# An adaLN, recurrence and gated-RNN kernel in f32: three tiny tensors declared behind the weights, so that the weights begin at multiples of 128 bytes

## What is computed

```python
xb = jnp.einsum('bsd,ed->sbe', x, B)
def step(h, xb_t):
    h = jnp.tanh(h @ A.T + xb_t)
    return (h, h @ C.T)
out = jnp.transpose(ys, (1, 0, 2)) + x            # then normalised, * gamma + beta

def step(c, xt):
    ft = jax.nn.sigmoid(xt @ wf.T + c @ uf.T + bf)
    it = jax.nn.sigmoid(xt @ wi.T + c @ ui.T + bi)
    gt = jnp.tanh(xt @ wc.T + c @ uc.T + bc)
    c = ft * c + it * gt
    return (c, None)
h = jnp.tanh(jnp.einsum('tbi,oi->tbo', x, wo) + c_final @ uo.T + bo)

h = _layernorm(x) * (1 + ca) + sa
x = x + ga * _L0_attn_ref(h, ...)
h = _layernorm(x) * (1 + cb) + sb
x = x + gb * _L0_ffn_ref(h, ...)
```

## The kernel before

| tensor | before | of 128 | changed | of 128 |
|---|---|---|---|---|
| ident | 16512 | 0 | 16512 | 0 |
| ones, mhalf, epst | 17024, 17056, 17088 | 0, 32, 64 | 54592, 54624, 54656 | 64, 96, 0 |
| AT | 17120 | 96 | 17024 | 0 |
| uoT | 19168 | 96 | 19072 | 0 |
| 16 split weights, 2048 bytes each | 21216 to 51936 | 96 | 21120 to 51840 | 0 |
| cb1T, sbT, biasT and other small ones | 53984 to 54624 | | 53888 to 54528 | |
| state | 54688 | 32 | 54688 | 32 |
| hsh, hsl, hs, hi, lo | 120224 to 161184 | 32 | the same | 32 |
| xn2, cst, chi, clo, uvec, tA and the rest | | 32 | the same | 32 |

## Time and profile before

### The profile page before, as it was taken

The page is one execution under the profiler, slowest core; times in us unless marked ns, Lnnn a source line. Parts: engine busy times, 40 slices in busy tenths (PEclk is TensorE's granted clock), DMA queues, the critical chain, the costliest instruction groups (busy, mean ns, idle before and its releaser), DMA issues.

```text
span 557.4 us, 13414 instructions
## 1 busy us (share of the span) xinstructions
PE 541.2 (97%) x4612; PEld 530.3 (95%) x4612; DVE 393.7 (71%) x910; ACT 341.6 (61%) x862; POOL 345.8 (62%) x475
## 2 busy tenths in 40 slices
PE   6999999999999999999999999999999999999994
PEld 3899999999999999999999999999999999998984
DVE  5989878885767665555866676776667676686664
ACT  3777777775466555465765556666665556666651
POOL 4767777670375444454776666677666757768444
PEclk9999999999999999999999999999999999999998
DMA  8666444435243222222133333343333333423234
GB/s 277 179 208 198 136 141 152 139 98 154 84 138 103 72 70 77 77 67 77 58 105 103 102 105 92 122 117 113 96 95 96 95 96 99 125 80 110 68 117 152
DMA packets 58513, 64.08 MB, mean 115 GB/s; under 512 B 5408, under 2 KB 49736, under 8 KB 58448
## 3 DMA queue, kind: packets, MB, share of 16 engines
q1 hardware_dynamic: 58448, 63.26, 36.9%
HBM read 46.44 MB, written 16.81 MB: 113 GB/s over the span
## 4 chain that ended last, share of the span: by engine, by line
PE 81%; POOL 6%; issue 4%; DVE 3%; ACT 3%; DMA 1%; SPq 0%; POOLq 0%; DVEq 0%; ACTq 0%
PE psOF L1589 11%; PE psI L1589 11%; PE psG L1589 11%; PE psWR L1548 7%; PE psWR L1647 6%; PE psWR L1493 4%; PE psOF L1493 4%; PE psC L1575 4%; PE psWR L1457 4%; PE psOF L1457 4%; PE psOF L1575 3%; PE psT L1626 2%; POOL wx L705 2%; PE psWR L1532 1%; PE psOF L1532 1%
## 5 line engine op out<-in xcount | busy, mean ns | idle before, releaser
L649 POOL TENSOR_TENSOR hin<-hin,uvec 128x256 f32<-128x256 f32 x64 | 51.8, 830 | 29.8 <-ACT hin L813 27.8
L656 POOL TENSOR_TENSOR hsl<-hs,hsh 128x512 fp32r<-128x512 f32 x24 | 31.0, 1291 | 49.1 <-DVE state L1313 32.7
L1294 DVE SCALAR_TENSOR_TENSOR lo<-psT,cb1T,hi 128x256 fp32r<-128x256 f32 x60 | 26.3, 479 | 42.0 <-ACT hi L878 41.9
L690 POOL TENSOR_TENSOR zn<-zn,tA 128x512 f32<-128x512 f32 x32 | 46.2, 1442 | 11.1 <-ACT zn L851 11.1
L1162 DVE TENSOR_TENSOR pre<-psWR,state 128x256 f32<-128x256 f32 x44 | 18.5, 421 | 46.4 <-PE psWR L1548 46.1
L851 ACT ACTIVATE zn<-state,nmA,rstdA 128x256 f32<-128x256 f32 x64 | 35.0, 594 | 26.2 <-POOL nmA L680 26.2
L1548 PE MATMUL psWR<-hs,AT 128*128 128x128 f32 x368 | 49.5, 274 | 0.2 <-ACT hs L837 0.2
L663 POOL TENSOR_TENSOR xin<-xin,tA 128x512 f32<-128x512 f32 x32 | 41.3, 1290 | 13.1 <-DMA tA<-rows_d 13.1
L840 ACT ACTIVATE hs<-pre 128x256 f32<-128x256 f32 x44 | 18.4, 417 | 50.6 <-DVE pre L1162 50.3
L1106 DVE SCALAR_TENSOR_TENSOR hin<-xin,mvA,uvec 128x256 f32<-128x256 f32 x56 | 41.5, 780 | 8.9 <-DMA h_park<-hin 8.4
L1548 PEld LDWEIGHTS psWR<-hs,AT 128*128 128x128 f32 x368 | 45.2, 191 | 0.4 <-ACT hs L837 0.3
(11 more groups left out here) (385 smaller groups left out, 2337.6 us busy)
## 6 DMA issues: line engine op xcount, KB each, us to landing
h_park<-hin SPq DMA_DIRECT2D x32, 256.0 KB, 2.2
hin<-h_park SPq DMA_DIRECT2D x64, 128.0 KB
xin<-in_L_attn_x_dram SPq DMA_DIRECT2D x64, 128.0 KB
tA<-rows_d SPq DMA_DIRECT2D x32, 256.0 KB, 4.6
out_dram<-state SPq DMA_DIRECT2D x64, 128.0 KB
xin<-in_L_attn_x_dram SPq DMA_DIRECT2D x28, 256.0 KB, 2.9
tW<-rows_d SPq DMA_DIRECT2D x32, 128.0 KB, 3.2
tG<-rows_d SPq DMA_DIRECT2D x24, 128.0 KB, 3.8
```

What stands on the lines that cost most here:

```text
L649: pool.tensor_tensor(h, h, sa, ALU.add).then_inc(a_h, 1)
L690: pool.tensor_tensor(two(zn[:, :]), two(zn[:, :]), both(tA[:, m % 2, 0:D]), ALU.mult).then_inc(s_zg, 1)
```

## The change

The three tensors `ones`, `mhalf` and `epst` are declared behind the weights and their small companions and ahead of `state`. AT, uoT and the split weights, 36 KB in each partition, move down by 96 bytes, and so do the small tensors behind them; the three take the 96 bytes ahead of `state`. From `state` on nothing moves. No instruction is added, removed or moved on any engine; only addresses differ.

```diff
         ident = sb("ident", [P, P])
-        ones = sb("ones", [P, 1])
-        mhalf = sb("mhalf", [P, 2])
-        epst = sb("epst", [P, 2])
         AT = sb("AT", [P, H, D])
         uoT = sb("uoT", [P, H, D])
         SPLIT = ["C", "wf", "wi", "wc", "uf", "ui", "uc", "wo"]
...
+        ones = sb("ones", [P, 1])
+        mhalf = sb("mhalf", [P, 2])
+        epst = sb("epst", [P, 2])
         state = sb("state", [P, PAIRS * W])
```

## The result

The changed kernel takes 567.09 us (566.78 to 567.20, four runs) against 559.89 us for the kernel before in the same comparison (559.58 to 560.29): 1.0127 times as long, with a 95% interval of 1.0115 to 1.0139, or 7.2 us more. The forecast was 555.0 us with a range up to 560.3. It was wrong in its sign.

The account below looks back on a forecast made before the run. TensorE's matmul start distances bound the kernel. Gains in L1575 (2.46 + 0.30), L1647 (1.13 + 0.85), L1669 and L1680 (0.17) made 4.9 us, 4.8 after a loss: 559.85 - 4.8 = 555.05, forecast 555.0, range 552.6 to 560.3.

Parts of the forecast that it names:

- What bounds the kernel: Whole kernel: TensorE, busy 541.2 of 557.4 us; time is nearly the sum of distances between matmul starts.
- The seventeenth piece: f32r matmuls: a moving operand begun at byte 32 of 64 touches 17 pieces, not 16, costing 272 cycles, not 256.
- the first rival: All f32r matmuls: the 16 extra cycles are a fixed price whatever the start; 559.7 us, chance 0.26.
- So it hangs on the moving side: f32r matmuls: only the moving operand's start matters, judged from L1669 and L1680; the gates keep 113.3 ns.
- The sum: L1575, L1647, L1669 and L1680: aligned moving weights go at 109.2 ns; together 4.9 us less, 4.8 after a loss.
- A rule against a row: f32r rows: beyond a fixed 2.5 ns per matmul they hold 4.2 ns that an aligned start could give back.
- The terms put at nothing: AT in the f32 recurrence, the first pass's L1493 and uoT: the change alters nothing there.
- The wide kind takes over the gates: Gates: 1,767 narrow distances become wide, 7.8 us more; 567.5 us, or 562.8 with the forecast's gain; chance 0.11.
- Nothing moves: All f32r matmuls: 16 cycles are a fixed price, starts at multiples of 32 change nothing; 559.7 us, chance 0.26.
- the slower case: Gates: their narrow distances become wide, giving 567.5 or 562.8 us; chance 0.11, outside the range.

Follow-up runs that it names:

- e1: Changed kernel with 32 empty bytes ahead of `state`; 563.30 us, 1.0066 of the kernel before.
- e6: Changed kernel with 160 empty bytes ahead of `state`; 560.93 us, 1.0022 of the kernel before.
- e7: Kernel before with B kept 64 bytes further on in chi and clo, which moved clo by 128 bytes; 562.38 us, 1.0044 of the kernel before.
- e9: Kernel before with B kept 64 bytes further on in chi and clo, clo moving by 256 bytes; 558.42 us, 0.9970 of the kernel before.
- e10: Kernel before with only the weights of C and wo at their places in the changed kernel; 563.74 us, 1.0061 of the kernel before.
- e2: Kernel before with 64 empty bytes ahead of `state`; 573.59 us, 1.0252 of the kernel before.
- e12: e2 with the gates' stationary operand cut from 128 to 32 columns in five of six matmuls; 568.06 us, 1.0142 of the kernel before.
- e5: Kernel before with 64 empty bytes ahead of `AT`; 560.34 us, 1.0013 of the kernel before.
- e14: e9 with the weights of C and wo 128 bytes further on; 561.24 us, 1.0029 of the kernel before.

## Why the prediction was wrong

**What bounds the kernel: right.** The span followed the sum of TensorE's start distances in every run, and lies 0.3 to 1.4 us above what that sum gives from the kernel before. In the changed kernel the summed distances account for 6.5 of 7.0 us of span, and no other engine's waits came into it.

**The seventeenth piece: wrong, and the root of the rest.** "At 16 cycles a piece that is 272. I take this as the reading." The 272 cycles are there with an aligned moving operand too: L1669 after the change at 113, and every narrow group of e1 and e6, where both sides begin at a multiple of 64. In all sixteen traces no f32r distance settles below 113.3. The arithmetic fitted to 0.1 ns and was chance, which the first rival said in so many words. As far as these runs go, 16 cycles are what an f32r matmul of 256 columns pays, wherever its operands begin. I had no aligned f32r row, said so, and still gave the reading 0.54 on the strength of a fit with one point.

**"So it hangs on the moving side": wrong as concluded, from a row that was read right.** The 8-column loads show that the 6.7 ns don't need a long load. They say nothing of what a long load adds in other places, and their 113.3 was itself one of several paces that they can have (116.7 in e7 and e9, with the same operands at the same bytes). I took "the narrow kind does not need it" for "the start of the stationary side does not matter". The gates were the term that I put at nothing, and they cost 5.0 us.

**The sum: its sign fell.** L1575 and L1647, for which I had counted a gain of 4.7 us, lost 0.3 and 1.2 (e10: the same 0.3 and 1.2 with only their weights moved). The 109.2 ns that the sum put in for an aligned weight is shown by no f32r row of any run, so the 4.2 ns of "A rule against a row" were there to be given back nowhere. The terms put at nothing for the recurrence (L1548 and L1457, 0.0 us), for B (0.0) and for uo (0.0) were right.

**The rival that came.** "The wide kind takes over the gates", with + 7.8 us. The evidence for it was in the text: L1493, with both sides at the same byte of 128, wide in all its groups. What I set against it, that narrow and wide stand in one pair of operands and go by what stood ahead, is true and no argument: for the lines with long loads the starts give the kinds, what stood ahead picks one (e2 has no narrow group of gates at all; e10 has both at unchanged starts). Its mechanism was right in that the distance of the two starts decides; the kind that the gates went into is not the old wide one, 117.8, but one of 116.9 on the mean that mostly steps 113, 116, 118, 120; and 1.2 us of the sum are L1647's and 0.3 L1575's. That its 567.5 lies 0.4 from the measured 567.1 is luck: the gates cost 5.0 us and not 7.8, and L1647, L1575 and the end of the kernel, at which it had nothing, made up the rest. It deserved a good part of the 0.54.

**"Nothing moves": half right.** That rival had the 16 cycles right as a price that an aligned start doesn't take away, and the time wrong: with every start at a multiple of 32 before and after, the change cost 7.2 us and e2 14.3.

**The range.** It took in a gain that rested on one reading, and the case of nothing; the slower case was left out as part of 0.20.

What stays open: the mechanism, and whether it is a collision of the two reads at all. By D alone the kinds are ordered for seven values (0: 120.0; 128: 118.7; 80: 118.7; 32: 118.2; 224: 117.0; 64 and 192: 113.3 or 117.8), but not explained, and in e12 half of it or more stays with five loads in six short. The shift rows at 120.0 in e2 and e12, with their own operands unmoved, say that the D of what ran just before counts too; no run moves the operands of the recurrence alone, which would tell how much. A group's own D counts too: in e7 the recurrence kept its D of 64, and the move of clo alone took the gates on chi and clo from 113.8 to 117.7. What sets a group narrow or wide at 64 and 192 isn't settled either: e5 and e6 keep about the shares of the kernel before, e14 lost them for C and wo and for the gates behind them.

## What to carry to other kernels

Where TensorE is full with f32r matmuls and a load for each, compare the start bytes of each matmul's stationary and moving operand, in the built program, before anything else is tuned: on this kernel 96 bytes fewer ahead of the weights cost 1.3%, 64 bytes more ahead of the states 2.5%, and B begun 64 bytes further on gained 0.3%. For the gates a distance of 64 modulo 256 was the best of seven; given to C and wo as well (e14) it cost 2.8 us. Rounding starts to 64 or 128 did nothing by itself. After any change of the declarations look at the distances of the timeline again, since a new tensor of 32 bytes moves all that follows it. And a reading that fits one value to a tenth of a nanosecond needs a second value that it could have missed.

## What the runs showed of the hardware beyond that

- With nothing changed but a start, f32r matmuls of 256 columns and 128-column loads stand 113.3 to 120.0 ns apart. This speaks against the read of the moving operand and the load of the stationary one being free of each other. The Trainium skill, "SBUF — State Buffer", section "Who interferes with whom", gives TensorE two SBUF read ports, one for the moving operand and one for the loads, and calls them independent. e2 and e12 don't fit that: 64 bytes of shift cost 14.3 us, and with five in six of the gates' loads cut to a quarter of their length 5.5 of them go.
- f32 products are nearly free of it: transposes (L1626) at 109.0 to 109.3 ns in all of the traces, uo at 215.4 to 216.0, the recurrence at 111.0 to 111.7, with the upper values in e2 and e12, where D is 0.
- A stream of f32r matmuls can stand at two paces with the same operands, 113.3 and 117.8 ns, and in the kernel before keeps the wide one over all 72 matmuls of a group of gates (from 484 us) and into the product by wo behind it. A change of line can also end it, as at the gates behind 21 of its projections.
